# Between two attentions: the first queries one place forward, the last queries' deviations on GpSimd

## The reference, cut to what matters

```python
x = _layernorm(x + _L0_attn_ref(x, ...), axis=-1)
x = _layernorm(x + _L0_xattn_ref(x, ctx_1024, ...), axis=-1)
x = _layernorm(x + _L0_ffn_ref(x, ...), axis=-1)

def _L0_xattn_ref(x_query, x_context, Wq, Wkv, Wp, bp, ln_g, ln_b):
    q = (x_query @ Wq).reshape(B, Nq, H, D).transpose(0, 2, 1, 3)     # H = 16 heads of D = 8
    ...
    q = layernorm(q, ln_g, ln_b)      # over the 8 elements of each head
    k = layernorm(k, ln_g, ln_b)
    q = q * SCALE
    attn = jnp.einsum('bhqd,bhkd->bhqk', q, k)
    attn = jax.nn.softmax(attn, axis=-1)
    out = jnp.einsum('bhqk,bhkd->bhqd', attn, v)
    ...
    return out @ Wp + bp
```

## Time and profile before

| | us |
|---|---|
| median of 3 runs | 418.78 |
| lowest, highest | 417.75, 419.29 |
| profiled execution, its own time | 420.02 |
| its span, first to last instruction | 418.2 |

### The profile page before, as it was taken

One profiled execution on the slowest core, in us unless ns is written; L12 is line 12 of the kernel. 1 busy time (PEld: TensorE's weight loads), 2 busy tenths in 40 slices (PEclk: granted clock), 3 DMA queues, 4 the chain that ended last, 5 costly groups with the idle time before them and its releaser, 6 DMA issues.

```text
span 418.2 us, 9993 instructions
## 1 busy us (share of the span) xinstructions
PE 381.3 (91%) x4008; PEld 258.8 (62%) x4008; DVE 273.0 (65%) x704; ACT 234.4 (56%) x442; POOL 130.5 (31%) x126
## 2 busy tenths in 40 slices
PE   4989996798999999999999999899998999999991
PEld 2556683566766847566667778446776466666671
DVE  6778877535657586779898885634666544444446
ACT  2855568656677267889999971235556432222210
POOL 6939932101331330028789780100012000000001
PEclk9999999869999999999999999999999999999998
DMA  6320000000000000112323210720000000000001
GB/s 178 80 52 2 4 2 2 2 2 2 5 1 2 0 2 2 63 56 78 105 84 112 77 38 2 241 61 3 3 4 2 0 2 0 0 2 1 2 0 50
DMA packets 16881, 13.84 MB, mean 33 GB/s; under 512 B 6548, under 2 KB 14133, under 8 KB 16837
## 3 DMA queue, kind: packets, MB, share of 16 engines
q1 hardware_dynamic: 15538, 12.51, 10.1%
q10 hardware_dynamic: 1299, 0.71, 0.6%
HBM read 12.64 MB, written 0.57 MB: 32 GB/s over the span
## 4 chain that ended last, share of the span: by engine, by line
PE 78%; ACT 9%; DVE 7%; issue 3%; DMA 1%; POOL 0%; POOLq 0%; DVEq 0%; ACTq 0%
PE PS L1923 10%; PE PS L1993 7%; PE PS L1494 7%; PE PS L1997 7%; PE PS L2024 6%; PE PS L1434 5%; PE PS L1910 4%; PE PS L1473 4%; PE PS L1514 4%; ACT att L655 3%; PE PS L1440 2%; PE PS L1566 2%; PE PS L1724 2%; PE PS L1429 2%; PE PS L1497 2%
## 5 line engine op out<-in xcount | busy, mean ns | idle before, releaser
L655 ACT ACTIVATE att<-PS 77x512 f32<-77x512 f32 (+1 forms) x96 | 51.6, 591 | 43.5 <-PE PS L1497 43.5
L982 DVE TENSOR_REDUCE mxp<-PS 128x4 f32<-128x308 f32 (+1 forms) x96 | 48.0, 536 | 32.3 <-PE PS L1473 32.2
L902 ACT ACTIVATE kM<-PS 128x512 f32<-128x512 f32 x32 | 19.1, 597 | 55.5 <-PE PS L1993 54.4
L511 POOL TENSOR_TENSOR rstd<-ve,neg_half 128x1 f32<-128x1 f32 x24 | 14.0, 585 | 108.3 <-DVE ve L976 108.3
L1306 DVE TENSOR_TENSOR_SCAN big<-big,PS 128x768 f32<-128x768 f32 x22 | 38.3, 1748 | 6.1 <-PE PS L1910 5.7
L1373 DVE TENSOR_TENSOR big<-kM,PS 128x512 f32<-128x512 f32 x32 | 21.9, 687 | 27.3 <-PE PS L1997 26.1
L505 POOL TENSOR_TENSOR rstd<-ve,neg_half 128x4 f32<-128x4 f32 x6 | 6.2, 1030 | 102.5 <-DVE ve L932 102.5
L1993 PE MATMUL PS<-xT,V 128*128 128x512 f32 x64 | 33.0, 596 | 1.1 <-DVE xT L1361 0.8
L1997 PE MATMUL PS<-xT,V 128*128 128x512 f32 x64 | 32.7, 592 | 0.0
L2024 PEld LDWEIGHTS PS<-big 128*128 128x128 f32 x256 | 29.7, 192 | 3.3 <-issue 3.3
L2024 PE MATMUL PS<-big 128*128 128x128 f32 x256 | 29.7, 275 | 0.0
(11 more groups left out here) (362 smaller groups left out, 862.5 us busy)
## 6 DMA issues: line engine op xcount, KB each, us to landing
kM<-Cdram SPq DMA_DIRECT2D x6, 384.0 KB, 3.5
XH<-Cdram SPq DMA_DIRECT2D x5, 384.0 KB, 3.5
xT<-Cdram SPq DMA_DIRECT2D x5, 384.0 KB, 3.3
V<-in_L_ffn_Wg SPq DMA_DIRECT2D x1, 1024.0 KB, 5.5
V<-in_L_ffn_Wu SPq DMA_DIRECT2D x1, 1024.0 KB, 8.1
out_x<-X SPq DMA_DIRECT2D x2, 256.0 KB, 2.3
ctxN<-in_ctx ACTq DMA_DIRECT2D x1, 308.0 KB
X<-in_x SPq DMA_DIRECT2D x1, 256.0 KB, 3.8
```

Of the source, the lines that this page charges most:

```text
L655: A_(PT[0:nk, i % 2, g], bank4(at.bank("exp", i, g), nk), ACT.Exp, scale=at.scale)\
L982: V_.tensor_reduce(mxp[:, b % 3, g, 0:J], PS[:, at.bank("max", b, g), 0:J * nk].rearrange("p (j k) -> p j k", j=J), axis=AX.X, op=ALU.max) ...
```

## The change

It moves work of the stretch between `at1` and `at2` to other places and other engines; what is computed stays the same.

1. Batches 0 to 3 one place forward. Their turning (`x1T.0`) goes from step 8 of `at1` to step 7, their product `q2.0` from step 9 to step 8. For that DVE applies batch 3 at the end of step 6 (this holds for all three attentions), and the norm of the keys (L964) goes from step 6 to step 5. The end of `at1` on DVE is written out as `first_half_between`; the end of the other attentions, `last_batches`, now takes the statistics of a batch ahead of the application of the batch before. Four `keep_busy` matmuls are added in step 8.
2. The turned queries 0 to 3 go to two banks and are copied in two halves; the second half of the keys is copied wholly after them.
3. Batches 4 to 7: `q2.1` becomes a bank of ACT. ACT squares it to `sq`, copies it to `qc` with a second instruction, and has no root and no table loads there. DVE sums the squares and adds epsilon. POOL raises 128x16 numbers per batch to the power -1/2, four instructions, behind the two residual sums of `at2`. DVE multiplies one batch at the end of each of steps 0 to 3, from SBUF, and PE's transpose of a late batch waits for it. The turning `x1T.1` and the product `q2.1` now stand ahead of the first shifted scores.

```diff
@@ POOL
+        pool.wait_ge(event("q_ss"), 2)
+        for b in range(HB, B):
+            n = slice(b * H, (b + 1) * H)
+            P_.tensor_tensor(out=hr1[:, n], in0=hvar[:, n], in1=half_bh[:, 0:H], op=ALU.pow).then_inc(event("q_rstd"), 1)
@@ ACT
-        attention_scalar(at1, {0: lambda: context_copies(3), B: x1_half, B + 1: queries_keys})
-        act.wait_ge(event("q2T_ready"), 1)
-        A_(half(qT, 0), bank4(Q2T_BANK), ACT.Identity, scale=gb2[:, 0:1], bias=gb2[:, 1:2]).then_inc(event("q2T_copied"), 1)
-        key2_copies(1, [1, 2, 3]).then_inc(aring.copied, 1)
+        attention_scalar(at1, {0: lambda: context_copies(3), B - 1: lambda: copy_out("x1T.0", half(xT, 0), bank4),
+                               B: first_queries, B + 1: lambda: key2_copies(0, [1, 2, 3]).then_inc(aring.copied, 1)})
+        for p in range(2):
+            h = slice(2 * p, 2 * p + 2)
+            act.wait_ge(event("q2T_ready"), p + 1)
+            A_(qT[:, h, :], bank4(Q2T_BANKS[p])[:, h, :], ACT.Identity, scale=gb2[:, 0:1], bias=gb2[:, 1:2])\
+                .then_inc(event("q2T_copied"), 1)
+        aring.take(act, "k2.1")
+        key2_copies(1, range(J)).then_inc(aring.copied, 1)
         table(ACT.Exp)
-        def late_deviations():
-            table(ACT.Sqrt)
-            query_deviations(1)
-            table(ACT.Exp)
+        copy_out("x1T.1", half(xT, 1), bank4)
+        def second_squares():
+            i = aring.take(act, "q2.1")
+            A_(half(sq, 1), bank4(i), ACT.Square).then_inc(event("q_sq"), 1)
+        def second_queries():
+            A_(half(qc, 1), bank4(aring.place[aring.index["q2.1"]]), ACT.Copy).then_inc(aring.copied, 1)
@@ DVE
+        def late_query(b):
+            dve.wait_ge(event("q_rstd"), b - HB + 1)
+            aring.wait_copied(dve, "q2.1")
+            q = qc[:, b, :].rearrange("p (h d) -> p h d", d=HD)
+            V_.tensor_tensor(q, q, hr1[:, b * H:(b + 1) * H].rearrange("p (h o) -> p h o", o=1).to_broadcast([128, H, HD]),
+                             ALU.mult).then_inc(event("q_normed"), 1)
+        def first_half_between(at):
+            residual(at, 5)
+            statistics(at, 5)
+            query_variances(0)
+            apply(at, 4)
+            normalise(at, 7, inverse(at, 7))
+            residual(at, 6)
+            first_queries()
+            statistics(at, 6)
+            residual(at, 7)
+            statistics(at, 7)
+            apply(at, 5)
+            apply(at, 6)
-        attention_vector(at1, {0: key_variances, 2: weights2, 3: weights5, 6: keys_normed},
-                         stats_after={B + 1: first_variances, B + 2: first_queries})
-        attention_vector(at2, {}, {0: late_queries})
+        attention_vector(at1, {0: key_variances, 2: weights2, 3: weights5, 5: keys_normed}, ending=first_half_between)
+        attention_vector(at2, {-1: lambda: query_variances(1), **{b - HB: lambda b=b: late_query(b) for b in range(HB, B)}},
+                         {-2: lambda: apply(at1, B - 1)})
@@ PE
                 if at.late and 1 <= i <= HB:
+                    pe.wait_ge(event("q_normed"), i)
                     nc.tensor.transpose(PS[:, bank, 3 * T:4 * T], qc[:, HB + i - 1, :], ident[:])
@@
             keys_turned(0)
+            at1.wait_flip_read(pe, B - 1)
+            keep_busy(Q2T_BANKS[0], 4)
@@
-        attention_tensor(at1, {B: first_keys, B + 1: first_queries}, 0,
-                         [keys_ready, contexts, values_copied, lambda: None, last_context], {B: x1_half})
-        at1.wait_flip_read(pe, B - 1)
-        keep_busy(Q2T_BANK, 8)
+        attention_tensor(at1, {B: first_keys, B + 1: lambda: keys_turned(1)}, 0,
+                         [keys_ready, contexts, values_copied, lambda: None, last_context],
+                         {B - 1: x1_half, B: lambda: queries(dring, 0)})
+        keep_busy(Q2T_BANKS[0], 8)
         dring.wait_copied(pe, "q2.0")
@@
+        def second_half_turned():
+            aring.wait_copied(pe, "k2.1")
+            keep_busy(at2.bank("flip", -1), 4)
+            pe.wait_ge(event("q2T_copied"), 2)
+            transposed_half("x1T", 1, X[1], at1.x_ready, HB)
-        query_opening = [queries_turned, lambda: None, keys_copied, lambda: transposed_half("x1T", 1, X[1], at1.x_ready, HB),
-                         late_queries]
+        query_opening = [lambda: queries_turned(1), lambda: None, second_half_turned, second_queries, lambda: None]
```

More of the change, by code:

```diff
@@ L714, in key2_copies, with first_queries @@
             return ins
-        def x1_half():
-            copy_out("x1T.0", half(xT, 0), bank4)
+        def key2_copies(c, js):
+            for j in js:
+                ins = A_(kM2[:, j, c * HB:(c + 1) * HB, :], bank_ctx(aring.place[aring.index[f"k2.{c}"]]), ACT.Identity,
+                         scale=sc2[:, j:j + 1], bias=sh2[:, j:j + 1])
+            return ins
+        def first_queries():
+            act.wait_ge(dring.full, dring.index["q2.0"] + 1)
+            A_(half(qc, 0), bank4(dring.place[dring.index["q2.0"]]), ACT.Square).then_inc(event("q_sq"), 1)
+            table(ACT.Sqrt)
+            act.wait_ge(event("q_ss"), 1)
+            A_(hr0[:, 0:HB * H], hss[:, 0:HB * H], ACT.Sqrt, scale=1.0 / HD, bias=eps_col[:]).then_inc(event("q_std"), 1)
             act.wait_ge(event("small"), 2)
@@ L967, in head_scale, with statistics @@
                              ALU.mult).then_inc(event(done), 1)
[L969 to L976 removed]
+        def statistics(at, r):
+            dve.wait_ge(at.residual_ready, r + 1)
+            step(V_.bn_stats(st[:, r, :], R[:, r, :]))
+            step(V_.bn_aggr(mv[:, r, :], st[:, r, :]))
+            V_.tensor_scalar(ve[:, r:r + 1], mv[:, r, 1:2], EPS, None, ALU.add).then_inc(at.eps_ready, 1)
@@ new lines, in apply, with residual @@
+        def apply(at, b):
+            dve.wait_ge(at.rstd_ready, b + 1)
+            V_.tensor_scalar(at.Xout[:, b, :], R[:, b, :], mv[:, b, 0:1], rstd[:, b:b + 1],
+                             ALU.subtract, ALU.mult).then_inc(at.x_ready, 1)
+        def residual(at, r):
+            i = r + 3
+            dve.wait_ge(at.proj_ready, r + 1)
+            if i < B + 2:
+                dve.wait_ge(at.flipped_copied, i + 2)
+            if at.late and i <= HB:
+                dve.wait_ge(at.late, i)
+            if r == 0 and not at.masked:
+                dve.wait_ge(at.xb_ready, 2 if at.late else 1)
+            V_.tensor_tensor(R[:, r, :], at.XB[:, r, :], PS[:, at.bank("flip", i), 2 * T:3 * T], ALU.add)\
+                .then_inc(at.residual_ready, 1)
@@ new lines, in normalise, with last_batches @@
+        def normalise(at, n, inverted):
+            dve.wait_ge(dve_step.sem, inverted)
+            if n >= 2:
+                dve.wait_ge(at.flipped_ready, n + 2)
+            V_.tensor_tensor(oN[:, n % 2, :].rearrange("p (h d) -> p h d", h=H), out_heads(at, n)[:, :, 0:HD],
+                             rs[:, n % 2, :].rearrange("p (h o) -> p h o", o=1).to_broadcast([128, H, HD]),
+                             ALU.mult).then_inc(at.normed, 1)
+        def last_batches(at):
+            for i in range(B, B + 4):
+                r, b, n = i - 3, i - 4, i - 1
+                if r < B:
+                    residual(at, r)
+                if n < B:
+                    normalise(at, n, inverse(at, n))
+                if r < B:
+                    statistics(at, r)
+                apply(at, b)
@@ L993, in remainder @@
                                  ALU.subtract).then_inc(at.part_ready, 1)
-            for i in range(-2, B + 4):
-                ahead, done, added, left = i + 2 < B, 0 <= i - 1 < B, 0 <= i - 3 < B, 0 <= i - 4 < B
+            for i in range(-2, B):
+                ahead, done, added, left = i + 2 < B, 0 <= i - 1, 0 <= i - 3, 0 <= i - 4 < B - 5
                 b, n, r = i - 4, i - 1, i - 3
                 if added:
[L999 to L1009, removed]
+                    residual(at, r)
                 if ahead:
@@ L1012, in attention_vector @@
                 if done:
[L1013 to L1022, removed]
+                    inverted = inverse(at, n)
                 if ahead:
```

135 lines of the change are left out of this document (59 added, 76 removed).

## The result

| | median us | lowest to highest | runs |
|---|---|---|---|
| before | 418.71 | 417.22 to 420.28 | 20 |
| after | 420.58 | 416.51 to 421.9 | 20 |

(One far outlier of each, at 644.66 and 766.15 us, is left out of the spans.) The ratio after to before is 1.004, 95% interval 1.0022 to 1.0057: the kernel became 1.9 us slower by the medians, where 2.0 us less were forecast. By the bound of 0.5% it counts as no change; the interval lies on the slow side all the same. The profiled execution of after took 420.62 us (span 418.8, mean clock 0.975).

A forecast was written before the change was run, and what follows sets the result against it. PE bounds the kernel, busy 91% of the span, losing time in gaps and the slow-clock stretches after them. Gain -3.5 plus clock +1.5 gives -2.0 us: 418.0 profiled, 416.8 us median; range 415.0 to 419.3.

The forecast's parts named there:

- The forward move: Batches 0 to 3, end of `at1`: reciprocal at 66.1, queries ready at 68.15 (gain 0.8 us), residual 7 done at 68.95.
- Eight fillers: PE behind its wait for residual 7: fillers issue for 1.75 us, so queries are turned at 70.7 against 69.02.
- The clock's cost: Opening of `at2`: one half-speed stretch over fillers and scores, taken as 1.5 us, partly absorbed by fillers and waits.
- rival B: Two slow stretches or one longer: 3 us cost, 418.3 us; usual runs before may lose less; 0.28 including D.
- The sign that I had named: TensorE's clock at half beyond 85 us would make the forecast wrong.
- The hand count: PE up to weigh(1) at full clock: scores 71.8, weigh(0) 82.9, weigh(1) 87.5 against 91.05, gaining 3.5 us.
- From the profile to the median: Profiled 420.02 us becomes 418.0; the same difference on the median 418.78 gives 416.8 us.
- The late norm: Late queries, batches 4 to 7: removing ACT's root and table loads ends the 2.46 us gap ahead of weigh(0).
- POOL's powers: Late batches' powers on POOL: 2.9 us each, bounds 2.9 and 4.8; hidden, but the first by nothing.
- D: Powers take 4.8 us, so the first late batch waits: +1.1 us, perhaps the clock too, 418 us; 0.28 with rival B.
- Rival C: DVE's late multiplications and POOL's powers block each other over SBUF: +3.7 us, 422.5 us; chance 0.08.
- Rival A: Clock stays full in the opening, or dips where PE waits anyway: -3.5 us, 415.3 us; chance 0.19.

The follow-up runs named there:

- the kernel with residual 7 first: Kernel after with DVE's residual 7 moved ahead of the first queries' root-dependent steps and multiplication: median 415.82 us, ratio 0.9953 to before.
- the nine fillers alone: Kernel after plus three filler matmuls in each of three short TensorE waits of `at2`, gap kept: median 417.33 us, ratio 0.9983 to before.
- the late part alone: Kernel after with queries 0 to 3, keys' norm and DVE's last steps ordered as before; POOL's powers, copies, shorter opening kept: 416.97 us, ratio 0.9977.
- the fillers in the gap: Kernel after with the eight fillers put ahead of TensorE's wait for residual 7 instead of behind it: median 421.42 us, runs 413.39 to 422.12.
- the best of the kernels: Kernel after with residual 7 ahead of the first queries' steps, plus nine fillers in three short TensorE waits: median 413.16 us, ratio 0.9897 to before.

## Why the prediction was wrong, step by step

- *The forward move.* Right almost to the tenth: reciprocal at 66.11, queries ready 68.16, residual 7 done at 68.96, gap of 2.62 us.
- *Eight fillers, 1.75 us.* Wrong in size: from their start to the turning it was 72.40 - 69.02 = 3.38 us (3.59 with the last one's end), at half clock. The turning came at 72.40, not 70.7.
- *The clock's cost, 1.5 us in one stretch.* This is the step that failed. There were two slow stretches, as in rival B, and they cost 3.1 us up to weigh 1. The measure is the kernel with residual 7 first, which ran this part at full clock: from the first filler to the turning it took 1.96 us where the kernel after took 3.38, from there to the scores 1.19 against 1.38, and from the scores to weigh 1 16.18 against 17.66. So 1.6 us went in the first stretch and 1.5 in the second, where the nine fillers alone gave 1.4 to 1.8. I took 1.5 for everything, out of bounds of 0 to 4.1, because fillers and waits would absorb part; but from 69 to 74 us TensorE's work, fillers and turning, was itself the path, and nothing absorbed it. The sign that I had named came: half clock beyond 85 us, to 87.4.
- *The hand count.* Against its full-clock course (scores 71.8, weigh 0 82.9, weigh 1 87.5) after stood at 73.78, 86.20 and 91.44, so 2.0, 3.3 and 3.9 us late. Of the 3.9, 3.1 are the clock; the count itself was 0.8 short. A forecast gain of 3.5 us and 3.9 us lost make 0.4 us later than in before, which is what the profiled pair shows at weigh 1.
- *From the profile to the median.* Also wrong. I carried the difference of -2.0 over unchanged. But the profiled run of before stood 1.3 us above the median of its 20 runs (420.02 against 418.71), that of after at its own (420.62 against 420.58): the pair differs by 0.6 us, the medians by 1.9. My -3.5 also contained the price of both falls of that run of before; its second profile had one, and weigh 1 stood at 87.97 there, 3.1 us earlier. Rival B's last sentence said so, and I gave it no number.
- *The late norm.* Right in kind: no gap ahead of `weigh`. Its worth alone, together with the half copies and the shorter opening, is 1.2 us of median (the upper end of the interval is 0.9999).
- *POOL's powers.* Right: 11.52 / 4 = 2.88 us each. D is out.
- *Rival C.* Out for these pairs: of the first three multiplications, 0.28 us each, two (at 85.14 and 91.50) stood inside the powers' time, 81.50 to 93.02. But the same pair of engines met where I had not looked: POOL's addition stretched DVE's write to 1.18 us and pushed two maxima back. The Trainium skill ("SBUF — State Buffer", Who interferes with whom) names `tensor_scalar` among the operations that can take the port pair shared with GpSimd, and lets the later one block. For this pair the trace agrees: 1.18 us against 0.35, begun 0.17 us behind POOL's addition and ended 0.08 us behind it. For DVE's two-input multiplication beside a power, of which the prediction had the same section's rule, it does not (0.28 us).
- *Rival A*, full clock, 415.3 us, had the right mechanism for another kernel: with residual 7 first, 415.82. That the numbers are so near is luck: that kernel has no late fillers, weigh 1 at 86.12 and not 87.5, and a fall at 170 us.

What cost the time was the order on DVE: 0.29 us of residual, on which TensorE's next work hung, behind 2.5 us of queries and statistics. Whether the forward move is worth having without that is not shown: with residual 7 first the median is 1.15 us below that of the late part alone, in the same series, and the two intervals overlap (0.9929 to 0.9977, 0.9954 to 0.9999).

## What to carry to other kernels

When a change moves work on one engine, look for what else waits behind that work: here a short add that released TensorE cost 4.2 to 4.8 us where it stood and nothing one block earlier. Price a gap of TensorE by the time that the work behind it takes at half clock, on the path, and not by the gap; and compare two profiles of the unchanged kernel before taking a slow stretch for its normal state. Independent matmuls in short waits cost nothing here, and the best of the kernels, 413.16 us and 1.0% under before (0.987 to 0.9925), has them.

## What the runs showed of the hardware

- One program has several times, by how often the clock falls: with the fillers in the gap 413.39 us at 0.994 and 422.12 at 0.966, no instruction changed.
- The same 0.80 us busy in a stretch of 2 us was followed by a fall at 70 to 72 us with the fillers in the gap, and by none at 78 to 80 us with residual 7 first. Nor does one program behave alike: in before, 0.91 us busy in 70 to 72 us was followed by a fall at 73 us in one profile, and 0.81 by none until 83 us in the other, behind the gap. What decides between them these runs do not tell.
- An addition of POOL, both inputs in SBUF, held DVE's `tensor_scalar` (SBUF to SBUF) for some 0.8 us, and left the reductions from PSUM alone (four in 1.63 us beside it and without it).
